# Output products of the local attention layers with 32 instead of 64 stationary columns

## The reference, cut to what matters

```python
WINDOW = 32; HEADS = 16; DIM_HEAD = 64; DEPTH = 6
def local_attention(q, k, v):            # b, h, n, d
    ...                                   # windows of 32 queries
    bk2, bv2 = (look(bk), look(bv))       # each sees its own and the previous window
    sim = jnp.einsum('bhwie,bhwje->bhwij', bq, bk2) * QK_SCALE
    sim = jnp.where(mask, -jnp.finfo(sim.dtype).max, sim)
    attn = jax.nn.softmax(sim, -1)
    out = jnp.einsum('bhwij,bhwje->bhwie', attn, bv2)
    return out.reshape(b, h, n, d)
def attn_layer(x, Wqkv, qs, ksc, Wo):
    q, k, v = jnp.split(x @ Wqkv, 3, -1)
    ...                                   # l2norm, scales, rotary
    return local_attention(q, k, v) ... @ Wo
for i in range(DEPTH):
    x = attn_layer(shift_tokens(x), ...) + x
    x = ffn_layer(shift_tokens(x), ...) + x
```

## Time and profile before

| | us |
|---|---|
| median of 3 runs | 2627.02 |
| lowest, highest | 2624.55, 2627.31 |
| the profiled execution, whole | 2627.24 |
| its span, first to last instruction | 2625.4 |
| from the first `score` (L1148) to the last | 573.3 to 2261.8 |

### The profile page before, as it was taken

One profiled execution on the slowest core, in us unless ns is written; L12 is line 12 of the kernel. 1 busy time (PEld: TensorE's weight loads), 2 busy tenths in 40 slices (PEclk: granted clock), 3 DMA queues, 4 the chain that ended last, 5 costly groups with the idle time before them and its releaser, 6 DMA issues.

```text
span 2625.4 us, 98068 instructions
## 1 busy us (share of the span) xinstructions
PE 2457.4 (94%) x36441; PEld 1721.1 (66%) x36441; DVE 2001.0 (76%) x4387; ACT 1889.6 (72%) x6630; POOL 1761.6 (67%) x1605
## 2 busy tenths in 40 slices
PE   6999799978999999999999999999999999789999
PEld 5888454545666666666666666666666666468884
DVE  5555499976888888888888888888888888565544
ACT  4777588856788888878888888888788888533323
POOL 1788766547788888878888888887878887312200
PEclk8999799989999999999999999999999999899999
DMA  4101200021111111121112111211112111100000
GB/s 118 15 15 15 49 12 11 11 70 29 31 33 50 47 41 34 32 64 40 33 33 61 39 39 33 56 41 41 33 40 57 41 33 33 36 1 1 1 1 16
DMA packets 176292, 91.06 MB, mean 35 GB/s; under 512 B 40926, under 2 KB 172232, under 8 KB 175824
## 3 DMA queue, kind: packets, MB, share of 16 engines
q1 hardware_dynamic: 167200, 80.50, 11.4%
q0 software_dynamic: 8192, 4.21, 1.4%
q10 hardware_dynamic: 432, 0.07, 0.0%
HBM read 30.57 MB, written 3.76 MB: 13 GB/s over the span
## 4 chain that ended last, share of the span: by engine, by line
DMA 28%; PE 26%; SPq 24%; DVE 9%; issue 6%; POOL 5%; ACT 1%; another core or an unknown queue 1%; DVEq 0%; POOLq 0%; ACTq 0%
DMA rg_prod<-vt 26%; SPq L556 23%; DVE rg_prod L952 3%; POOL rs L1549 2%; PE scores L654 2%; PE bank L1114 2%; PE bank L626 1%; PE bank L1847 1%; PE bank L1871 1%; POOL t_pair L1539 1%; PE bank L2104 1%; PE bank L1841 1%; PE bank L1865 1%; PE bank L1131 1%; PE bank L675 1%
## 5 line engine op out<-in xcount | busy, mean ns | idle before, releaser
L1549 POOL TENSOR_TENSOR rs<-ssc,neg_half 128x8 f32<-128x8 f32 x384 | 647.5, 1686 | 43.5 <-DVE ssc L1370 43.5
L1477 ACT ACTIVATE pr<-scores,negmax 128x64 f32<-128x64 f32 x1536 | 461.7, 313 | 59.9 <-DVE negmax L1378 34.1
L1539 POOL TENSOR_TENSOR t_pair<-qn_pair,tabs 128x512 f32<-128x512 f32 x384 | 489.2, 1274 | 13.1 <-DVE qn_pair L1358 12.5
L1529 POOL TENSOR_TENSOR pr<-pr,rec 128x256 f32<-128x256 f32 x384 | 235.7, 614 | 314.4 <-DVE rec L1350 314.2
L1114 PE MATMUL bank<-wqk,xs 128*128 128x512 f32 x768 | 407.1, 612 | 22.8 <-DVE qn_pair L1358 19.2
L1013 POOL DMA_INDIRECT rg_win<-rg_images,share_down x256 | 250.4, 978 | 117.9 <-DVE rg_prod L952 61.9
L1477 ACT ACTIVATION_READ_ACCUMULATOR pr<-scores,negmax 128x1 f32 x1536 | 311.5, 203 | 0.0
L1468 ACT COPY vt<-bank 128x256 f32<-128x256 f32 x361 | 135.1, 374 | 208.9 <-issue 113.5
L1366 DVE TENSOR_REDUCE ss<-sq 128x8 f32<-128x512 f32 x384 | 261.1, 680 | 31.9 <-ACT sq L1500 30.8
L1358 DVE TENSOR_TENSOR qn_pair<-bank,rs 128x512 f32<-128x512 f32 x384 | 257.7, 671 | 29.3 <-POOL rs L1549 29.0
L1131 PE MATMUL bank<-oT,wo 128*128 128x128 f32 x1536 | 266.7, 296 | 0.0
(11 more groups left out here) (307 smaller groups left out, 5541.9 us busy)
## 6 DMA issues: line engine op xcount, KB each, us to landing
rg_prod<-vt SPq DMA_DIRECT2D x1536, 32.0 KB
wqk<-in_L_ffn_Wqkv SPq DMA_DIRECT2D x20, 256.0 KB
rg_win<-rg_images,share_down POOLq DMA_INDIRECT x256
wv<-in_L_ffn_Wqkv SPq DMA_DIRECT2D x20, 128.0 KB
wo<-in_L_ffn_Wo SPq DMA_DIRECT2D x20, 128.0 KB
w<-in_L_ffn_W SPq DMA_DIRECT2D x6, 341.0 KB
rg_images<-rg_prod SPq DMA_DIRECT2D x1, 1625.0 KB, 8.9
rg_images<-XT SPq DMA_DIRECT2D x16, 64.0 KB
```

What stands on the lines that cost most here:

```text
L1477: ex = act.activation(pr[t % 2][:, h * BAND:(h + 1) * BAND], sl_ps[:, h // 2, h % 2 * BAND:(h % 2 + 1) * BAND], ACT.Exp, bias=negmax[t % 2 ...
L1539: pool.tensor_tensor(t2[t % 2][:, :].rearrange("p (i h f e) -> p i h f e", i=2, h=GH, f=2), qn[t % 2][:, :].rearrange("p (i h f e) -> p i ...
L1549: pool.tensor_tensor(rs[t % 2][:, :], ssc[t % 2][:, :], neg_half[:, 0:8], ALU.pow)\
```

## The change

The two loops over the column halves `r` of 64 become one loop over four parts of 32 columns. Each product keeps its 64 rows and its span of queries, and has half as many stationary columns; there are 24 in place of 12. Which probabilities are read (`r * P + lo`) follows from `r = part // 2`. The values read and the rows written are those of before, in pieces of 32.

```diff
                 for k, (_, lo, hi) in enumerate(SPANS):
-                    for r in range(2):
+                    for part in range(GV // 2 // WINDOW):
+                        r = part // 2
                         for pair in range(2):
                             row = slice(pair * HD, (pair + 1) * HD)
-                            at = SLOT_V[k][pair] * P + r * HD
+                            at = SLOT_V[k][pair] * P + part * WINDOW
                             values = vt[t % 3] if k == 2 * pair else vx[t % 2]
-                            mm = pe.matmul(ol_ps[r * HD:(r + 1) * HD, pair, lo:hi], values[row, at:at + HD],
-                                           pT[t % 2][row, r * P + lo:r * P + hi],
+                            mm = pe.matmul(ol_ps[part * WINDOW:(part + 1) * WINDOW, pair, lo:hi],
+                                           values[row, at:at + WINDOW], pT[t % 2][row, r * P + lo:r * P + hi],
                                            start=True, stop=True, skip_group_check=True)
                 mm.then_inc(a.o_ready, 1)
```

## The result

The changed kernel takes 2685.19 us (median of 4 runs, 2679.72 to 2688.54) where the kernel before takes 2627.16: a ratio of 1.021, 95% interval 1.0192 to 1.0228, so 58 us slower. Later, with other runs of before beside it, the ratio was 1.0187 (1.0151 to 1.0223). The forecast was 33 us slower, 2660; the measured time lies above the 2680 up to which the forecast itself reached and 0.8 us under the upper end of the range, 2686.

What follows compares the result with a forecast made beforehand. The prediction took SP's serial pass of transfers, waiting for its own landings, as the bound: 58 us for added instruction packets less 25 us of regained waits, 33 us slower, 2660 us; forecast 2635 to 2680, 8-in-10 range 2620 to 2686.

Steps and rivals of the forecast that it cites:

- SP is the bound and waits for itself: Local layers: SP's queue stands at L554 for its own last transfers in 320 of 333 passes, 4.38 us a tick.
- Each packet costs SP's pass 0.87 us: SP's passes in the local layers: 67 more 16 KB packets of PE instructions on q8 at 0.87 us, 58 us slower.
- cheap packets: Rival at SP's passes: an added packet costs at most 0.43 us, giving 2626, or 2602 at no cost; chance 0.14.
- dear ones: Rival at SP's passes: each added packet costs 1.57 us, 80 us slower, 2707; chance 0.06.
- SP regains 25 us of waits: SP's waits for PE and ACT from 700 to 2260 us: 25 of 30 us go.
- `attend` ends 0.13 us earlier: On PE each tick, the 0.14 us turn from score goes and 48 records take 0.37 us; 34 us if PE were bound.
- the signs to look for: Local layers: 0.80 q8 packets a tick, passes 3.72 us without one, last score to first attend start under 0.02 us.
- My bounds: For attend's end on PE: 0.10 to 0.15 us earlier near score's step, 0.21 us later at 14 ns a record.
- The rival that the change does not do what it says: On PE the turn stays or the step is 14 ns, attend ends 0.07 to 0.21 us later, 2685; inside the forecast.
- The sum: Whole kernel: 58 us for packets less 25 us of SP's waits regained, 33 us slower, 2660.
- PE's wait at `attend` grows from 18.7 to some 80 us: PE at attend's line in the local layers: waits some 0.24 us a tick where it waited 0.06.
- The first rival: PE pays out: SP's passes shrink with PE, its 34 us come through, 2593, if mean pass under 4.23 us; chance 0.10.

Runs made afterwards that it cites:

- the form with 16 products: Changed kernel with the two short query spans taken as one, so attend issues 16 products: 1.0008 of before; 0.9824 with two semaphores for the landings.
- the kernels with two semaphores: Two semaphores for v_spread landings, taken in turn, so SP need not await its last landing: kernel before 2580.25 us (0.9913), changed kernel 2598.07 us (0.9988).
- the four forms: attend with 12 products (kernel before), 16, 20 (16 with four issued twice) and 24 (changed kernel); one-semaphore local stretches 1688.3, 1682.8, 1730.3, 1744.4 us.

## Why the prediction was right, and where not

*SP is the bound and waits for itself:* right. Taking only that wait away gave about 20 us to the kernel before and about 60 to the changed one, and PE's gain in the form with 16 products did not come through.

*Each packet costs SP's pass 0.87 us:* right in kind and size. Passes without one stayed at 3.75, with one at 4.6 us in both, 0.84 and 0.90 apart, and the kernels with two semaphores show no such step. The number came out as said, 0.80 a tick. The rivals of cheap packets, 0.43, and of dear ones, 1.57, fall with that. What lengthens the pass is still only known by coincidence in time, in hundreds of passes, and by the number of passes with a packet in the four forms; no run moved the packets to another moment and left all else.

*SP regains 25 us of waits:* too high. Between 800 and 2260 us its waits for PE, ACT and DVE at L554 and L556 did vanish (13.9 to 0.2), but 5.0 us of waiting for PE at L562 came up, where it had been 0.8. Between 700 and 800, 11.1 of the 17.5 us stayed: there PE was the later of the two and, with a longer `attend`, not earlier than before. The 49th pass began at 797.7 us before and at 798.7 after. So some 15 us were regained, 9 or 10 of them behind the 49th pass.

*`attend` ends 0.13 us earlier:* the step that failed. The turn gave 0.07 of its 0.14 and did not go: of the signs to look for, under 0.02 us between the last `score` and the first `attend` record came in none of the 332 ticks. The 24 products took 0.47 and not 0.37 us. I had taken the pace of `score`, 7.7 ns a record, for a pace that PE can hold. `attend` ends about 0.08 us later. My bounds (0.10 to 0.15 earlier, 0.21 later) held it only because I kept the far end. With SP off the path this costs 19.7 us.

*The rival that the change does not do what it says* had `attend` end 0.07 to 0.21 us later, which is what came, and it gave 2685 us, which is what was measured. That agreement is luck: the 2685 was reckoned from the far end, 0.21, with PE's side as the bound. At 0.08 later PE's side would need 4.40 us a tick, less than SP's 4.55, and SP stayed the bound. The range, too, held by 0.8 us only.

*The sum:* from the 49th pass to the 383rd SP's passes sum to 1463.2 us before and 1519.3 after, 56.1 more. The 64 packets more at 0.87 are 56, less 9 or 10 regained is 46 or 47. The missing 10 are not settled. The price of a packet is not known well enough for it: from the groups above it comes out between 0.80 and 0.90 us in six traces with one semaphore, and each of these is sure to some 0.07 only; 0.04 more or less on 267 packets is 11 us. Ticks of over 6 us, from one `score` to the next, were one in the kernel before and three in the changed one, of 8.5 to 8.7 us, each at a load of the feed-forward weights; the chain has SP standing in the first of them for the landing of `w`:

```profile
951.10 4.24 DMA w<-in_L_ffn_W
...
957.16 3.57 DMA rg_prod<-vt
```

But the ten passes in which SP issues a load of `w` sum to 49.6 us before and 56.5 after, and all ten then have a packet, where six had one. So these loads hold 7 us at most, of which 3 or 4 are packets already counted.

*PE's wait at `attend` grows from 18.7 to some 80 us:* missed. Counted in the same way it is 35.1. The 18.7 leave out the waits of the weight loads in the same line, and the wait grew less than forecast because PE was 0.08 us later at the end of `attend` and not 0.13 earlier. By the starts of the records PE waits 0.07 us a tick before and 0.17 after, where the forecast had 0.06 and 0.24.

*The first rival*, that PE pays out, was wrong on both counts: its condition was a mean pass under 4.23 us, which is 4.55, and PE had nothing to pay.

## What to carry to other kernels

Before counting what an engine gains, look at whether some queue waits for its own last piece of work; here SP did so in 320 of 333 passes, behind a PE busy at 94%. In a program written out in full, instructions are transfers too: 18432 more on PE were 72 more packets of q8 here. They can slow a chain of small transfers that has nothing to do with them. A pace read from a short burst need not hold: `score`'s 16 products went at 15 ns each, `attend`'s 24 at 20. And two counts of a wait can be compared only if both take in the same instructions, matmuls alone or weight loads with them.

## What the runs showed of the hardware

An f32 product of 64 rows and 32 columns, two loads and two matmuls, came at 19.7 to 19.9 ns in `attend` with 24 or 16 of them and at 21.6 with 20, while the 16 of `score` took 15 ns each; what sets these paces was not tried. The turn between two blocks with equal places in the array was 0.08 to 0.09 us with nothing to wait for, against 0.146 between unequal ones: the drain that the Trainium skill names in "TensorEngine Tiling (Array Packing)", section "Key Properties", explains at most the 0.06 between them. An increment of a semaphore by PE cost 65 ns of its time. A pass of four 32 KB transfers that met a packet of 16 KB of instructions was 0.8 to 0.9 us longer. The Trainium skill, "Runtime: NRT & Kernel Launch", section "Instruction fetch mechanics", calls the cost of such a block mostly hidden; with two semaphores SP's passes follow PE, and those with and without a packet agree within 0.07 us, so little or nothing of it reaches PE; the transfers that it crosses do not go free.
